# The order of scores and weighted sums in a fused cross-attention and feed-forward kernel, and of three Vector steps in its first tile

## What is computed

```python
def _L0_xattn_ref(src, tgt, src_mask, tgt_mask, W_src, b_src, W_tgt, b_tgt, W_out, b_out):
    src_trans = (einsum('bsf,of->bso', src, W_src) + b_src) * src_mask[:, :, None]
    tgt_trans = (einsum('btf,of->bto', tgt, W_tgt) + b_tgt) * tgt_mask[:, :, None]
    src_key, src_val = split(src_trans, 2, axis=2)        # 8 heads of 32
    scores = einsum('bthd,bshd->bhts', q, k) / sqrt(HEAD_DIM)
    scores = where(src_mask[:, None, None, :] == 0, -inf, scores)
    tgt_update = einsum('bhts,bshd->bthd', softmax(scores), v)
    return einsum('btf,of->bto', concatenate([tgt, tgt_update], axis=2), W_out) + b_out

def _L0_ffn_ref(x, ...):                                   # weights w1, w2, h1, h2, w3 are -1, 0 or 1
    h = silu(_tlin(x, w1_w, w1_s)) * _tlin(x, w2_w, w2_s)  # 256 -> 1024
    h = gelu(_tlin(h, h1_w, h1_s)); h = gelu(_tlin(h, h2_w, h2_s))
    return _tlin(h, w3_w, w3_s)                            # 1024 -> 256

x = x + _L0_xattn_ref(ctx_2048, _layernorm(x), mask, mask, ...)
x = x + _L0_ffn_ref(_layernorm(x), ...)
```

## Time and profile before

| | us |
|---|---|
| median of three runs | 909.26 |
| lowest and highest | 908.71, 913.21 |
| profiled execution, its own time | 909.7 |
| span of its trace | 907.9 |
| PE busy (7600 matmul records) | 901.0 (99%) |
| PEld busy | 864.3 (95%) |
| DVE busy | 616.2 (68%) |
| ACT busy | 390.7 (43%) |
| POOL busy | 75.7 (8%) |

### The profile page before, as it was taken

The page is one execution under the profiler, slowest core; times in us unless marked ns, Lnnn a source line. Parts: engine busy times, 40 slices in busy tenths (PEclk is TensorE's granted clock), DMA queues, the critical chain, the costliest instruction groups (busy, mean ns, idle before and its releaser), DMA issues.

```text
span 907.9 us, 20852 instructions
## 1 busy us (share of the span) xinstructions
PE 901.0 (99%) x7600; PEld 864.3 (95%) x7600; DVE 616.2 (68%) x1224; ACT 390.7 (43%) x1100; POOL 75.7 (8%) x101
## 2 busy tenths in 40 slices
PE   9999999999999999999999999999999999999998
PEld 8889999999999999999999999999999999999998
DVE  6887858577575776757767576675857858576453
ACT  5872534435253252533526235252443524455231
POOL 3633000010000100001010010100001000000000
PEclk9999999999999999999999999999999999999999
DMA  9941132412314222142311324113241222303000
GB/s 350 380 120 45 60 95 69 121 49 74 85 51 121 58 96 65 41 121 69 103 53 35 121 69 121 35 51 105 69 121 46 72 75 67 92 23 106 25 13 14
DMA packets 82348, 79.20 MB, mean 87 GB/s; under 512 B 8592, under 2 KB 74896, under 8 KB 82320
## 3 DMA queue, kind: packets, MB, share of 16 engines
q1 hardware_dynamic: 81744, 78.31, 28.0%
q10 hardware_dynamic: 576, 0.52, 0.2%
HBM read 51.55 MB, written 27.26 MB: 87 GB/s over the span
## 4 chain that ended last, share of the span: by engine, by line
PE 94%; DVE 3%; issue 1%; POOL 1%; DMA 0%; ACT 0%; SPq 0%; DVEq 0%; POOLq 0%; ACTq 0%
PE F L627 58%; PE G L627 7%; PE F L738 7%; PE G L620 6%; PE G L478 5%; PE G L514 5%; PE G L496 2%; PE S L531 2%; PE G L603 2%; PE S L467 0%; DMA cT<-ctx_t 0%; DVE g L1237 0%; DVE mx L1115 0%; DVE pr L1108 0%; DVE mx L1087 0%
## 5 line engine op out<-in xcount | busy, mean ns | idle before, releaser
L854 ACT ACTIVATE g<-F,firsts 128x256 f32<-128x256 f32 x250 | 104.9, 472 | 314.6 <-PE F L627 314.4
L627 PE MATMUL F<-hBh,H 128*128 128x256 f32 x1008 | 239.2, 282 | 0.1
L627 PE MATMUL F<-hAh,H 128*128 128x256 f32 x992 | 235.8, 282 | 2.0 <-DVE flag L1280 2.0
L627 PE MATMUL F<-hBl,H 128*128 128x256 f32 x1008 | 236.2, 279 | 0.0
L627 PE MATMUL F<-hAl,H 128*128 128x256 f32 x992 | 233.0, 279 | 0.0
L627 PEld LDWEIGHTS F<-hBl,H 128*128 128x128 f32 x1008 | 190.0, 189 | 0.4
L627 PEld LDWEIGHTS F<-hBh,H 128*128 128x128 f32 x1008 | 188.9, 187 | 0.6 <-ACT g L854 0.3
L627 PEld LDWEIGHTS F<-hAh,H 128*128 128x128 f32 x992 | 186.1, 188 | 3.1 <-issue 2.3
L627 PEld LDWEIGHTS F<-hAl,H 128*128 128x128 f32 x992 | 186.8, 188 | 0.3
L1256 DVE CAST hBh<-g 128x512 fp32r<-128x512 f32 x64 | 28.5, 446 | 120.8 <-ACT g L854 120.8
L882 ACT ACTIVATE pr<-pr,nmx 128x128 f32<-128x128 f32 x240 | 92.7, 388 | 0.2
(11 more groups left out here) (160 smaller groups left out, 1504.3 us busy)
## 6 DMA issues: line engine op xcount, KB each, us to landing
p_dram<-pb SPq DMA_DIRECT2D x30, 512.0 KB, 3.3
pr<-p_dram SPq DMA_DIRECT2D x120, 128.0 KB, 3.2
H_raw<-h SPq DMA_DIRECT2D x16, 512.0 KB, 14.0
cT<-ctx_t SPq DMA_DIRECT2D x14, 512.0 KB, 3.3
x_dram<-xt SPq DMA_DIRECT2D x28, 256.0 KB, 2.3
out<-y SPq DMA_DIRECT2D x32, 128.0 KB, 1.7
x_in<-x_t SPq DMA_DIRECT2D x15, 256.0 KB, 2.7
x2T<-x_dram SPq DMA_DIRECT2D x60, 64.0 KB, 1.9
```

What stands on the lines that cost most here:

```text
L627: return mm(bank, W[0][:, k, cols], part[:, k, :], start=first, stop=last)
L854: fn(g[:, q % 2, m, :], mid_bank(f, q)[:, m, :], ACT.Gelu, scale=scols[:, col:col + 1]).then_inc(gelu_ready, 1)
```

## The change

In `middle_part`, `attend(a)` goes ahead of `scores(n)` in all tiles but the first. In tile 0, DVE does the gate product of quarter 2 before the split of quarter 1, and raises the second flag before the row maxima of the second sequence. Nothing is added or taken away.

```diff
@@ middle_part
+                first = isinstance(f, int) and f == 0
                 ends = isinstance(f, int) and f >= TILES - 2
                 for q in range(4, 12):
-                    if q == 8 and n is not None:
+                    if q == 8 and first:
                         scores(n)
                     if q == 8 and a is not None:
                         attend(a)
+                    if q == 8 and n is not None and not first:
+                        scores(n)
+                    if q == 8 and a is not None:
                         out_proj(a)
@@ tile, on VectorE
                 gate_times_up(f, 1)
-                split(f, 1)
-                gate_times_up(f, 2)
                 if first:
+                    gate_times_up(f, 2)
+                    split(f, 1)
                     row_max(1, 0)
+                else:
+                    split(f, 1)
+                    gate_times_up(f, 2)
                 gate_times_up(f, 3)
...
                     count_low_bits(1, CHUNKS)
+                    raise_flag(1)
                     row_max(1, 1)
-                    raise_flag(1)
```

## The result

| | before | after |
|---|---|---|
| median, us | 909.13 | 907.62 |
| lowest to highest, us (20 executions each) | 908.55 to 913.21 | 907.10 to 909.53 |
| profiled execution, us | 909.7 | 908.02 |
| its span, us | 907.9 | 906.2 |

A forecast was written before the change was run, and what follows sets the result against it. PE, busy in 99% of the span, bounds the kernel, so only its waits (4.6 us) or bad streaming can be won. -0.7 - 0.8 = -1.5 us from the profiled 909.7; against the median 909.26, 907.8 us, range 906.2 to 910.6.

The forecast's parts named there:

- Part 1: Tiles 1 to 13, sums ahead of scores: PE's wait for ACT's copy goes, 12 x 0.06 = 0.7 us less.
- The zero for the switches: Tiles 1 to 13: the new order of matmuls costs PE nothing; -1.3 and +1.3 us kept for the range.
- The margin of the probabilities: Sums ahead of scores need the turned probabilities sooner; their margin was over 4 us and is over 3.
- Part 2: Tile 0, flag and gate product sooner: of PE's 2.0 us flag wait only 0.88 pass, 0.8 us less.
- The cap by ACT: Tile 0: q = 6 waits for q = 4's gelu on busy ACT, so cannot start before 61.00 (was 61.88).
- What is late next: Tile 0: q = 8 needs the casts of chunks 18 and 19; 0.4 us are left even if they stay.
- Cap absent: Rival, tile 0: ACT gets earlier or q = 6 waits for less; whole 2.0 us pass, 906.6; chance 0.06.
- Flag held: Rival, tile 0: POOL holds the flag through its cast and two additions; 0.3 us worse there, 908.9; chance 0.08.
- No gain in the loop: Rival, loop tiles: ACT's copy is late for another reason, or switches eat the gain; 908.5; chance 0.08.
- slower switches: Rival, 13 swapped tiles: one more array drain each, 0.20 us a tile, 2.6 us in all, 910.4; chance 0.08.
- cheaper switch: Rival, swapped tiles: the new matmul order saves 1.3 us more, 906.5; chance 0.04.
- Late probabilities: Rival, 13 swapped tiles: transfers land over 3 us later, at most 1.1 us each, 922 us; chance 0.01.

The follow-up runs named there:

- e1: Kernel before with only the swap (weighted sums ahead of scores in tiles 1 to 13), DVE's order as before: 908.50 us, ratio 0.9956.
- e5: Kernel after with tile 1's scaling of `v`, done in tile 0, moved from ACT to DVE: 906.98 us, ratio 0.9930.
- e7: Kernel before with only the swap, plus tile 1's scaling of `v` moved from ACT to DVE, flag still late: 908.67 us, ratio 0.9991.
- e3: Kernel after without the sooner gate product (split of quarter 1 again ahead of the product of quarter 2): 907.58 us, ratio 0.9975.
- e9: Kernel after with weighted sums ahead of scores in tile 0 too: 908.68 us, ratio 0.9949.
- the first group: Four follow-up runs on one chip, sharing executions of the kernel before, whose median there was 913.37 us.
- e8: Kernel after with the second flag computed over two elements, in a tile of its own, instead of one: 906.65 us, ratio 0.9965.

## Why the prediction was right, point by point

**What bounds the kernel.** Confirmed in the main: of 4.6 us of waits in the earlier trace rows about a third reached the end, as worked out. "Or what it streams badly" was in the prediction too, but no term of the sum came from it, and the slow stretches are just that.

**Part 1.** The term of 12 x 0.06 = 0.7 us held to the digit: 3.71 us became 3.65 in each loop tile, and e1 showed it without the edits on DVE. Reading the loss from the start of the matmuls and not from the 2.3 us of the weight load's waits was what made it right. The zero for the switches held too (2.11 us from the sums to the projection). The step that is missing is the pace of the matmuls behind: 3 slow stretches of 0.14 us in the trace of before that are absent from the trace of after. They were there to be read, at 221.2, 443.7 and 666.1 us, and I had not compared the loop tiles with one another.

**The margin of the probabilities.** I put it at over 3 us from tile 1 alone. That holds in the loop. In tile 14, which has no scores and so no swap, it does not: the sums' weight load waits 0.2 us for `pr` in the profile of before and 0.4 in that of after, and most of the other profiles have no such wait. PE's own wait of 0.2 us for `pr` in the first view above is this one. "If PE waits for `pr`" was named as a sign of being wrong, and it did show, but in a tile that the change does not touch. The rival's chance was fair, but one tile is no bound for fifteen.

**Part 2.** The flag came at 51.1 (forecast 51.3), the look at 43.45 (43.6), q = 4 at 52.04 (52.3, just outside the 52.2 to 53.2 that was to show it), q = 6 at 60.74 (61.00) behind a wait of 0.99 us (0.5 to 1.2). The numbers are 0.22 us earlier than in the trace of before for a reason ahead of the change. The count of the low bits, ahead of the flag, is 0.18 us later against ACT's silus, where the forecast had 0.2 (the case in which `nmx` is let in). The gain at q = 6 was 0.92 us against 0.88. The cap by ACT, the step on which most hung, is what e5 and e7 show from two sides: with ACT relieved the wait goes and 0.65 us with it, and without the early flag nothing does. The gate product was rightly held to bring nothing, though by e3 it is lost ahead of q = 4 and not in the cap.

**What is late next.** I named the casts for q = 8 with 0.4 us left; no wait for them appeared. From 1.14 us at q = 6, 0.94 were left where tile 1 began (100.51 against 101.45). Of the 0.20 between, 0.12 are in q = 6 and 7, whose 64 matmuls take 7.74 us from the stalled one on where they took 7.62 before (the first is 0.11 us longer; I had 0.07), and 0.08 in the sums of tile 0, 1.09 us against 1.01. I had not listed these sums, and e9 shows that their transfers, which land near 69.9 us, are the nearer candidate. PE also waits 0.2 us for `kT` now, but ahead of q = 4, under the cap.

**The accounts.** From before's profile to after's: 0.94 us at the end of tile 0, of which 0.22 stand ahead of the change and 0.72 (forecast 0.8) are its own; at the keys of tile 13 (768.75 before, 766.67 after) 2.08 us, so the loop added 1.14, which is 0.72 and 3 x 0.14 = 0.42; at the last matmuls 1.68, as the last tiles took 0.4 back, most of it by the late transfer of tile 14. Without the 0.22 the change has 0.72 + 0.72 + 0.42 - 0.40 = 1.46 us. So the two terms of the sum make 1.44 of the 1.5, and were right for their own reasons; that the total agrees as closely as it does is luck, since 0.42 of slow stretches and 0.40 in the last tiles, neither of them in the sum, happened to cancel. Starts and ends differ by as much between executions of like code: q = 4 starts at 54.33 in the kernel before and at 53.82 in e1, whose tile 0 is the same.

**The range.** 906.2 to 910.6 was wide for an effect that came within 0.2 us, and right to be: the kernel before moved by more than the effect from one group to the next, in part through the two things that the prediction did not know, the low clock behind the flag and the slow stretches. That they explain the 913.37 us beside the first group is not shown. Both only make the kernel before slower, so the ratio leans to the gain where they are many: 0.9978 and 0.9966 for the same pair.

**The rivals.** Cap absent, 906.6: refuted by the 0.99 us wait. Flag held, 908.9: refuted for one element and true for two (e8). No gain in the loop, slower switches and cheaper switch: refuted by the 3.65 us blocks and the unchanged 1.0 and 1.1 us of sums and scores. Late probabilities: not in the loop, but in tile 0.

**A version that beats both.** The kernel after with the scaling of `v` on DVE (e5) took 906.98 us, 0.65 under the kernel after and a ratio of 0.9930 to the kernel before in its group, though that group's kernel before was a slow one; against 907.63 the ratio is 0.9993. It was not run in the same group as the kernel after. e8 has a lower median still (906.65), by the pace of its matmuls that nothing here explains, and not by anything that it was built for.

## What to carry to other kernels

When one wait is shortened, look for the next thing that the waiting engine needs and subtract only up to it: an engine that is busy without a gap up to that point is a cap, and it makes the sum safe from the details before it. Take the loss of a wait from where the matmuls start, not from the time that the weight load waited, and look through all tiles of the trace for equal blocks that take unequal time before pricing one of them. A wait of about 2 us on TensorE can cost again through the clock behind it, in some executions only, so a few executions of a kernel do not tell its time.

## What the chip did that I had not expected

- **Equal matmuls at two paces.** 128 matmuls of 256 columns took 14.93 or 15.08 us (116.7 or 117.8 ns each) at a granted clock of 1.00. With PE waiting 0.2 us for ACT in each loop tile, 3 to 16 of 28 or 29 stretches were slow; without, 0 or 1 in nine profiles, but 27 in the tenth, e8, whose gates' 16 matmuls were fast, 1.81 us against 1.87. The cause is open.
- **The clock behind a wait.** PE waited 2.0 us for the flag, and in 2 of 7 profiles then ran at 0.50 of full clock for about 3.3 us; no wait of 1.1 us at nearly the same place was followed by it.
- **One element is not held, two are.** DVE's `tensor_scalar` over one element ran its 0.14 us inside a cast on POOL; over two elements it took 2.33 us, through the cast and both additions that POOL had queued behind it.
